# A decoder layer in fp32: first maxima and last cross attention as 32-row tiles, one pool of PSUM banks, a new order of steps

## What is computed

```python
def attn(x):                       # self attention, causal; q, k, v and the output have biases
    scores = einsum('bntd,bnsd->bnts', q, k) / sqrt(8)
    scores = where(causal, scores, -inf)
    return softmax(scores) @ v @ Wp + bp
def xattn(x, ctx, mask):           # cross attention to 77 rows, masked
    scores = where(mask, -1e9, einsum('bhqd,bhkd->bhqk', q, k) / sqrt(8))
    return softmax(scores) @ v @ Wo.T
def ffn(x):                        # weights of the two best of 8 experts, from softmax(gate)
    y = einsum('bsd,edf->bsef', x, expert_W) + expert_b
    return einsum('bsef,bse->bsf', y, comb) / 2
x = x + attn(layernorm(x)); x = x + xattn(layernorm(x), ctx, mask); x = x + ffn(layernorm(x))
```

## Time and profile before

| | us |
|---|---|
| median of 3 runs | 418.57 (415.2 to 419.45) |
| the profiled execution | 416.35 |
| its span | 414.6 |

### The profile page before, as it was taken

One profiled execution on the slowest core, in us unless ns is written; L12 is line 12 of the kernel. 1 busy time (PEld: TensorE's weight loads), 2 busy tenths in 40 slices (PEclk: granted clock), 3 DMA queues, 4 the chain that ended last, 5 costly groups with the idle time before them and its releaser, 6 DMA issues. The chain is left out here.

```text
span 414.6 us, 6303 instructions
## 1 busy us (share of the span) xinstructions
PE 333.7 (80%) x2204; PEld 156.2 (38%) x2204; DVE 266.5 (64%) x655; ACT 178.0 (43%) x339; POOL 134.2 (32%) x199
## 2 busy tenths in 40 slices
PE   5944868999975498799879898997988859688883
PEld 1421423444442144346434443553442344332440
DVE  5835886786882288367999864897461268631377
ACT  1400243566575065587540577664059612018100
POOL 6550041232254031004538500332961123900014
PEclk9895786999999599899899989999799977769998
DMA  6861174000035320001541000002110002110000
GB/s 142 163 73 28 41 101 61 5 2 2 2 64 86 44 40 5 4 0 37 87 74 36 28 6 2 2 2 41 38 29 4 1 2 48 28 30 2 0 2 25
DMA packets 19637, 14.40 MB, mean 35 GB/s; under 512 B 2461, under 2 KB 19605, under 8 KB 19605
## 3 DMA queue, kind: packets, MB, share of 16 engines
q1 hardware_dynamic: 19149, 13.60, 18.6%
q10 hardware_dynamic: 456, 0.39, 0.4%
HBM read 2.45 MB, written 1.05 MB: 8 GB/s over the span
## 5 line engine op out<-in xcount | busy, mean ns | idle before, releaser
L788 DVE TENSOR_REDUCE peaks<-peak_ps 128x1 f32<-128x512 f32 (+3 forms) x176 | 106.8, 638 | 61.8 <-PE peak_ps L988 60.2
L692 ACT ACTIVATE probs<-unit_ps 128x512 f32<-128x512 f32 x160 | 87.6, 600 | 85.9 <-PE unit_ps L1025 85.5
L599 POOL TENSOR_SCALAR_AFFINE_SELECT probs<-probs 128x512 f32<-128x512 f32 (+1 forms) x80 | 43.9, 551 | 150.4 <-ACT probs L692 150.4
L988 PE MATMUL peak_ps<-k_stack,q_stack 96*128 96x512 bf16 (+2 forms) x192 | 68.4, 383 | 0.0
L979 PE MATMUL peak_ps<-causal,ident_b 128*128 128x128 bf16 (+2 forms) x176 | 47.7, 271 | 25.2 <-DMA k_stack<-parts_k 8.5
L1025 PE MATMUL unit_ps<-q_stack,k_stack 102*128 102x512 bf16 (+3 forms) x256 | 56.7, 309 | 4.2 <-ACT probs L692 1.9
L1040 PE MATMUL mix_ps<-probs,v_s 128*9 128x256 f32 (+3 forms) x512 | 45.8, 454 | 1.6 <-POOL probs L599 1.6
L979 PEld LDWEIGHTS peak_ps<-causal,ident_b 128*128 128x128 bf16 x176 | 17.7, 101 | 63.4 <-DVE peaks L788 37.4
L610 POOL TENSOR_TENSOR yw<-yw 128x512 f32<-128x512 f32 (+2 forms) x42 | 34.3, 816 | 17.2 <-DVE yw L876 13.9
L700 ACT ACTIVATE xprobs<-unit_ps 77x512 f32<-77x512 f32 x64 | 33.8, 594 | 11.0 <-PE unit_ps L1048 11.0
L1094 PE MATMUL unit_ps<-expert_w_s,normed_t 128*128 128x512 f32 x64 | 35.5, 673 | 1.6 <-DVE yw L876 1.3
(11 more groups left out here) (134 smaller groups left out, 407.8 us busy)
## 6 DMA issues: line engine op xcount, KB each, us to landing
q_stack<-parts_q SPq DMA_DIRECT2D x24, 128.0 KB, 3.9
k_stack<-parts_k SPq DMA_DIRECT2D x48, 64.0 KB
xq_stack<-parts_x SPq DMA_DIRECT2D x24, 128.0 KB, 3.8
state<-in_x SPq DMA_DIRECT2D x4, 256.0 KB, 5.7
out<-state SPq DMA_DIRECT2D x4, 256.0 KB, 2.3
expert_w_s<-in_expert_w SPq DMA_DIRECT2D x1, 512.0 KB, 5.6
xk_stack<-parts_x SPq DMA_DIRECT2D x12, 38.5 KB
q_stack<-peaks_t ACTq DMA_DIRECT2D x16, 12.0 KB
```

Of the source, the lines that this page charges most:

```text
L599: gp.affine_select(out=v, in_=v, compare_op=ALU.is_ge, fill=0.0, base=0, pattern=pattern, channel_multiplier=-1).then_inc(causal_done, 1)
L692: ac.activation(probs[:, grp % 2, u, :], unit_bank(step), ACT.Exp, scale=SCALE).then_inc(unit_taken[UNIT[step] % UNITS], 1)
L788: ve.tensor_reduce(dst, peak_bank(step)[:, 0:n * width].rearrange("p (h k) -> p h k", h=n), X_AXIS, ALU.max, negate=True).then_inc(peak_ta ...
L988: last = te.matmul(dst, q, keys, start=False, stop=(i == len(heads) - 1), skip_group_check=True)
```

## The change

- **Batch 0's maxima** (`TILED_PEAKS`) are made in fp32 without stacks. Weights in another column order (`wk_ts`, `wq_ts`, loaded first) put one head in each of four 32-row groups, with four groups of heads interleaved by 8 rows. ACT copies the projected keys once (`k_t`) and the projected queries four times (`q_t`), each time scaled by `own`, which is 1 on the 8 rows of the head that is meant and 0 elsewhere. `tile_peak` is then a matmul over 32 partitions, lane j = partitions 32j to 32j + 31, to a bank of its own; the causal bias is added by four bf16 matmuls of `pick` and `causal_rows`. There are 48 such steps and 64 reduces on DVE. The projections with their stacks are still made for the scores.
- **Batch 3's cross attention** (`TILED_CROSS`) has no stacks at all: `project_xt`, `tile_xpeak` (16 steps, four products of 77 columns each, one reduce), `turn_tile_xpeaks` (4, one for each group of four heads: PE turns the maxima, DVE adds them into a spare row of `xq_t`) and `tile_xscores` (16, fp32 over 32 rows). `context_tile` makes its keys once, early.
- **The mask** is -2^30, exact in bf16, in one row instead of three; 4 DMAs and five DVE instructions fewer.
- **Banks.** All eight PSUM banks are one pool; the planner gives each step its bank (`PLACE`), with a semaphore pair for each bank. `AHEAD` limits how many steps of a kind may be in flight in the plan.
- **The planner** has a new table of costs by engine, follows the four row tiles, banks and stacks, and takes from eight chains, `scores`, `experts`, `cross`, `scale`, `peaks`, `prepare`, `attend`, `context`, by the earliest start and then by that rank.
- **At the start** POOL clears `k_stack[:, 0]` only after the first x has been turned, DVE makes `lanes`, `pick` and `own` from the identity, `causal` is built before the steps, the weights for batch 0's tiles are loaded first, and warm matmuls write bank 7.

The core of the diff:

```diff
-UNITS, PEAK_BANKS = 3, 2
+BANKS, WARM_BANK = 8, 7
+TILE = 32
+SPARE = (16, 16, 0, 0)
+TILED_PEAKS, TILED_CROSS = 0, B - 1
+TILE_PEAKS = (((0, 0), (1, 128)), ((2, 0),), ((3, 0),))
+AHEAD = {'peak': 4, 'tile_peak': 3, 'xpeak': 2, 'tile_xpeak': 5, 'scores': 2, 'xscores': 5, 'tile_xscores': 5, 'expert': 5}
-ORDER = ("cross", "peaks", "experts", "prepare", "attend")
+ORDER = ('scores', 'experts', 'cross', 'scale', 'peaks', 'prepare', 'attend', 'context')
...
+LATENCY, HOP, SWITCH, RANK, ISSUE = 0.22, 0.05, 0.0, 0.0, 0.62
+        if kind in STACKS:
+            n, *counts = STACKS[kind]
...
+            for r, count in zip(ready, counts):
+                free["dma"] = max(free["dma"], r) + ISSUE * count
+            done[("stacked", -1 if kind == "split_context" else b, n)] = free["dma"] + 2.2
...
+                fit = [i for i in usable if bank_free[i] <= start]
+                i = max(fit, key=lambda i: bank_free[i]) if fit else min(usable, key=lambda i: bank_free[i])
+                bank_uses[i] += 1
+                place[step] = (i, bank_uses[i])
...
 SP, split_k of batch 0
                         wait_cleared(sp, "k_stack")
+                        for i in range(2):
+                            for s in range(2):
+                                r = MAX_ROW + 3 * s
+                                sp.dma_start(k_stack[r:r + 3, i, s], ones).then_inc(ones_stacked, 16)
...
 POOL
+                elif kind == "turn_x" and (b, k) == (0, 0):
+                    wait_taken(pool, step)
+                    gp.memset(k_stack[:, 0].bitcast(F32), 0.0).then_inc(cleared, 1)
...
 ACT
+                elif kind == "project_qt":
+                    act.wait_ge(bias_ready, 1)
+                    wait_full(act, step)
+                    for i in range(GROUPS):
+                        ac.activation(q_t[:, i], bank_of(step), ACT.Identity, bias=q_bias[:, i:i + 1],
+                                      scale=own[:, i:i + 1]).then_inc(q_ready if i < 3 else taken_of(step), 1)
...
 DVE
+                elif kind == "tile_peak":
+                    grp, i, j = k
+                    p, s = divmod(4 * grp + j, 2)
+                    wait_full(dve, step)
+                    for t, col in TILE_PEAKS[i]:
+                        last = ve.tensor_reduce(peaks[:, p // 4, t, p % 4, s:s + 1],
+                                                bank_of(step)[:, col:col + 128 * (t + 1)], X_AXIS, ALU.max, negate=True)
+                    last.then_inc(taken_of(step), 1)
+                elif kind == "turn_tile_xpeaks":
+                    wait_full(dve, step)
+                    ve.tensor_tensor(xq_t[:, k], xq_t[:, k], bank_of(step), ALU.add).then_inc(taken_of(step), 1)
...
 PE
+            def bank_free(step):
+                i, n = PLACE[step]
+                if i == WARM_BANK and n == 1:
+                    pe.wait_ge(causal_ready, 1)
+                if n > 1:
+                    pe.wait_ge(bank_taken[i], n - 1)
...
+                elif kind == "tile_peak":
...
+                    for c in range(4):
+                        te.matmul(diagonal, lane(pick, j)[:, 128 * c:128 * c + 128],
+                                  lane(causal_rows, j)[:, c].unsqueeze(1).broadcast_to([TILE, len(TILE_PEAKS[i]), 128]),
+                                  start=(c == 0), stop=False, skip_group_check=True)
+                    for t, col in TILE_PEAKS[i]:
+                        last = te.matmul(bank[:, col:col + 128 * (t + 1)], lane(q_t, j)[:, grp, 128 * t:128 * t + 128],
+                                         lane(k_t, j)[:, 0:128 * (t + 1)],
+                                         start=False, stop=(t, col) == TILE_PEAKS[i][-1], skip_group_check=True)
+                    last.then_inc(full_of(step), 1)
+                elif kind == "tile_xscores":
+                    grp, j = divmod(k, 4)
+                    if j == 0:
+                        wait_taken(pe, ("turn_tile_xpeaks", b, grp))
+                    bank_free(step)
+                    te.matmul(bank_of(step)[0:S2], lane(xk_t, j)[:, KEYS_OF[grp]], lane(xq_t, j)[:, grp],
+                              start=True, stop=True).then_inc(full_of(step), 1)
```

More of the change, by code:

```diff
@@ L178, in plan, with has_bank @@
+    return n.get(kind, lambda: [])()
+STACKS = {"split_q": ("q", 3, 2, 1), "split_k": ("k", 6, 4, 2), "split_xq": ("x", 3, 2, 1), "split_context": ("x", 6, 4, 2)}
 def plan():
     left = {name: list(steps) for name, steps in chains().items()}
-    ready = dict.fromkeys(ORDER, LOADED)
-    free = dict.fromkeys(("pe", "act", "dve", "pool", "dma"), 0.0)
-    banks = {"misc": [0.0] * 2, "unit": [0.0] * UNITS, "peak": [0.0] * PEAK_BANKS}
-    done, turned, norms, steps = {}, set(), [], []
+    free = dict.fromkeys(("act", "dve", "pool", "dma"), 0.0)
+    tiles, issue, mode = [0.0] * 4, 0.0, None
+    bank_free, bank_uses = [0.0] * BANKS, [0] * BANKS
+    done, begun, place, steps, norms, turned = {}, {}, {}, [], [], set()
+    ahead = {kind: [] for kind in AHEAD}
+    loaded = {("ln_stats", b, 0): (4.0, 13.0, 15.0, 17.0)[b] for b in range(B)}
+    loaded[("context_keys", 0, 0)] = 15.0
+    first, last = ("tile_peak", 0, (0, 0, 0)), ("tile_xpeak", B - 1, (3, 3))
+    def has_bank(step):
+        return cost(step)[0] and not (step[0] == "values" and step[2][1])
@@ L191, in plan @@
             kind = step[0]
-            pe, engine, busy, _ = cost(step)
-            if any(x not in done for x, _ in needs(step)):
+            if any(x not in done for x in needs(step)):
                 continue
@@ L197, in plan @@
                 continue
-            start = max([ready[name]] + [done[x] + delay for x, delay in needs(step)])
-            ring = ring_of(kind)
-            if ring:
-                start = max(start, min(banks[ring]))
-            start = max(start, free["pe"])
-            if best is None or start < best[0]:
-                best = (start, name, step, ring)
-        start, name, step, ring = best
+            pe = cost(step)[0]
+            start = max([loaded.get(step, 0.0)] + [done[x] for x in needs(step)])
@@ new lines, in plan @@
+            if pe:
+                tile = tile_of(step)
+                start = max(start, issue, max(tiles) if tile is None else tiles[tile])
+                if has_bank(step):
+                    usable = range(BANKS - (first not in done or last in done))
+                    start = max(start, min(bank_free[i] for i in usable))
+                if kind in AHEAD and len(ahead[kind]) >= AHEAD[kind]:
+                    start = max(start, ahead[kind][-AHEAD[kind]])
+            switch = bool(pe) and (tile_of(step) is None) != (mode is None)
@@ L206, in plan @@
+            key = (start + SWITCH * switch + RANK * rank, rank)
+            if best is None or key < best[0]:
+                best = (key, start, name, step)
+        _, start, name, step = best
         kind, b, k = step
-        pe, engine, busy, then = cost(step)
+        pe, work = cost(step)
         left[name].pop(0)
-        idle = int((start - free["pe"] - WARM_SLACK) / WARM_TIME)
-        if (("peak", 0, (0, 0)) not in done or ("split_xpeaks", B - 1, 0) in done) and idle > 0:
-            steps.append(("warm", len(steps), idle))
+        t = start
@@ new lines, in plan @@
+        if pe:
+            mode = tile_of(step)
+            idle = int((start - max(issue, max(tiles)) - 0.5) / 0.5)
+            if (first not in done or last in done) and idle > 0:
+                steps.append(("warm", len(steps), idle))
+            tile = tile_of(step)
+            t = start + pe
+            if tile is None:
+                tiles, issue = [t] * 4, t
+            else:
+                tiles[tile], issue = t, start + 0.05
+            t += LATENCY
+        made = []
+        for engine, busy, lag in work:
+            begin = max(free[engine], t)
+            free[engine] = begin + busy
+            t = begin + busy + lag
+            made.append(t)
+            t = t + HOP if engine == "pool" else begin + busy
@@ L235, in plan @@
+        if kind == "take_mix":
+            bank_free[place[("values", b, (k, 0))][0]] = t
+        if kind in AHEAD:
+            ahead[kind].append(t)
         if kind == "ln_norm":
@@ L712, in _ @@
+                    ac.copy(mixed_t[:, k], bank_of(step)).then_inc(taken_of(step), 1)
                 elif kind == "choose":
```

948 lines of the change are left out of this document (539 added, 409 removed).

## The result

The changed kernel takes 430.09 us (median of 4 runs, 426.95 to 431.62) against 419.01 of the kernel before beside it: 1.0275 times as long, with a 95% interval of 1.0185 to 1.0365. Its span is 429.6 us, 15 more than before, at a mean clock of 0.833 against 0.897. I had predicted 365 with a range of 338 to 398.

What follows compares the result with a forecast made beforehand. Nothing was at its limit from end to end: a stack-bound head, a middle with PE 87% busy, a one-chain tail. 414.6 - 24 - 18 - 11 = 361.6 us of span, 365.3 us as measured time, range 338 to 398.

Steps and rivals of the forecast that it cites:

- Head: Start of the kernel: batch 0's maxima without stacks let scores and batch 1 begin earlier, 24 us gained, bounds 15 and 33.
- 15.6 for all, half of DVE's, so it hides: Head: PE needs 3.9 us per four heads of batch 0's maxima, 15.6 in all, hidden under DVE's 31.2.
- Tail: Last batch's cross attention to the end: no x-query stacking and maxima turned by group, 18 us gained, bounds 8 and 28.
- 0.56 (maxima): Tail: PE's time for one group of cross maxima, within 3.9 us of PE work per group.
- the first cross scores come 3.5 us after the first maximum: Tail: maxima turned group by group shorten this from 14.4 us to 3.5, saving 10.9.
- four groups cost 4 us more: Tail: maxima running inside the cross attention lengthen each group from 2.92 to 3.9 us, if tiles run together.
- Middle: Between head and tail: one pool of eight banks lets PE run ahead, 11 us gained, bounds 15 lost and 30 gained.
- Switches: Tiling mode changes on PE: at most 48 at 0.25 us, 12 us, two thirds under DVE's pace in the head.
- Row tiles don't overlap: Rival, chance 0.08: batch 0's maxima cost PE up to 62 us, a tail group 8.3, total 399 us.
- The pool makes it slower: Rival, chance 0.09: PE waits in order for its planned bank while others are empty, time about 430 us.
- The middle becomes tight: Rival, chance 0.12: the middle's 33 us of idle and the cold stretches go nearly all, 342 us.
- my signs of being wrong: Batch 0's reduces wait for PE; a named bank often holds PE while others are free; last score no earlier than 305 us.

Runs made afterwards that it cites:

- e9: The changed kernel with the row-tiled queries and keys of both stages in bf16 instead of fp32: 388.8 us, 0.931 of the kernel before.
- e1: The changed kernel with batch 0's maxima and batch 3's cross attention back on stacks: 412.8 us, 0.986 of the kernel before.
- e6: e1 with the planner counting a stack as landed 6.9 us after its last issue, not 2.2: 398.5 us, 0.947 of the kernel before.
- e4: The changed kernel with three full-array bf16 products of 512 columns ahead of each four row-tiled steps: 435.4 us, 1.041 of the kernel before.
- e5: Matrix products alone, layer left out, row-tiled stretches between full-array fp32 ones: 32 records of 77 columns took 1.9 us at full clock, 3.7 at half.
- e15: Matrix products alone, layer left out, short and long forms on row tiles and full array: 77-column fp32 group 3.6 us on the full array.

## Why the prediction was wrong

**Head, predicted -24 us, measured +11.** The start came late, outside my bounds: the first tiled product at 15.8 against 12, and the first reduce at 17.1 against 12.4. The 3.6 us that x waits behind the warm matmuls aren't in my chain and are nearly all of it. The step that failed is "15.6 for all, half of DVE's, so it hides". A group of four heads was to cost PE 3.9 us; that holds when the form runs alone at full clock (three fours at 1.14 us). In the kernel a four takes PE 2.7 us at half clock, and scores and projections follow each: 3.7 us, some 11 to 12 a group. PE and not DVE set the pace, the 64 reduces ended at 83 us and not 48, and DVE was busy for 17.3 of the 32 us from 13 to 45, 0.54, where I had named over 0.9. From this the rest is late: the first score at 60 instead of 39, batch 1's first maximum at 88 instead of 58. That batch 0's stacks would be the next limit was never tested by the kernel: batch 1's last k copy was issued by 61.2, 26 us before its first maximum. The 6.9 us of landing that I took from the earlier trace rows are also uncertain, because four copies of ones into the same stack were issued behind the twelve, until 30.6.

**Tail, predicted -18 us, measured +36.** The x-query to its first use is 0.9 us, as predicted (1.2 against the 9.5 before). Then three terms failed. First, "0.56 (maxima)" for a group: I priced 308 fp32 columns by their columns, and the 32 weight loads alone are busy for 4.6 us. The first group takes 2.65 us and the later ones 4.8, together some 15 us more than I had. Second, "the first cross scores come 3.5 us after the first maximum": they come 350.7 - 335.5 = 15.2 us after the first product. The first reduce is released by POOL, after DVE has stood for 5.0 us: POOL clears the buffer of these maxima (L675) only behind the x-query, which isn't in my chain; then the second group, and batch 2's `add_attention` (2.1 us) with its turn stand ahead on PE. Third and largest, "four groups cost 4 us more". From the first cross scores to the residual add it was 17.1 us (371.4 to 388.5), would have been 21, and is 49.7 (350.7 to 400.4); before, and in the changed kernel:

```profile
388.51 0.69 DVE L829 TENSOR_TENSOR state<-misc_banks,state 128x512 f32<-128x512 f32 x1 [2.58 <-PE misc_banks L916]
```
```profile
385.53 4.35 PE L1304 MATMUL banks<-expert_w_s,normed_t 128*128 128x512 f32 x6
...
400.36 0.69 DVE L972 TENSOR_TENSOR state<-banks,state 128x512 f32<-128x512 f32 x1 [1.51 <-PE banks L1053]
```

In these 49.7 us lie two more groups of maxima, batch 2's gate and experts (L1304), and half clock for everything from 350 to 388 us. In e9 the same part takes 30.6 us. From the last self attention score to the x-query it takes 29 us and not 18, since batch 2's cross attention and experts stand there too. This is the work that left the middle: in e1, without tiles, the tail is already 113 us. So the tail of a stage cut at the last score is no measure of the last batch alone, and my 18 us were partly a matter of bookkeeping.

**Middle, predicted -11 us, measured -32.** The number flatters the forecast. PE is busy in the middle for 151 us where it was 178, a share of 85% in both and a clock of 0.93 in both: 27 of the 32 us are work that now lies in head and tail (1206 matmuls against 1343), and 5 us are less idle time. PE does meet a maximum's bank less often, but e1 gains 6 us in all by pool, order and mask, so my 11 for the middle was too much for this order; in e6's order the three together gain 20. The wait for batch 2's k_stack is there, at 3.9 us under the 5 I gave it; its last copy was issued by 135.8, so the landing took 7.6 us to the first use:

```profile
128.02 7.82 SPq L565 DMA_DIRECT2D k_stack<-parts_k  x12
...
143.40 0.58 PE L1167 MATMUL banks<-causal,ident_b 128*128 128x512 bf16 x1 [3.88 <-issue]
```

So PE is busy for 85% of the middle and not for 88 to 92%.

**Switches.** 0.25 us each, 12 us in all, most of it hidden. Measured 0.16 to 0.30 each; right in size, but not hidden, since PE was the slow side in the head. Up to 24 visits at 0.32 to 0.60 are 8 to 14 us. The sum had none of it.

**The rivals.** *Row tiles don't overlap* gave 62 us for the maxima and 8.3 for a tail group; measured 66 us (17 to 83) and 9. Its numbers came true and its mechanism is false: the tiles overlap, but they are slowed by half clock, by loads and by the work between. Its sum, 399 us, was still too low, as it left the head's and tail's other work at full clock. *The pool makes it slower* has the time (430) and the opposite mechanism. *The middle becomes tight* comes to 343 us and not 342. The clock was in no case: I read the earlier trace rows as saying that it falls where PE is idle. Two of my signs of being wrong came: the reduces of batch 0 wait for PE (31.8 us), and the last score is done at 306 us, not before 305.

## What to carry to other kernels

Price a matrix product by its weight loads and passes as well as its columns: 16 fp32 products of 77 columns cost 1.9 to 4.8 us of PE where their columns are worth half a microsecond, and in bf16 0.5. Before work is moved to an engine that seems half idle, add what the engine would have to do in that very stretch, at the lower clock too. One pool of banks was worth 25 us together with the order made for it, and an order made for a pool needs it. Check a planner's belief about when a transfer lands against the trace, and measure what a truer number brings: here it was 14 us in one order and nothing in another.

## What the hardware did that I had not expected

- TensorE was granted half clock with no idle time in the record, for 35.0 of 35 us in e4 and for 38 us in the changed kernel, the second by stage:

```profile
350.00:388.00 38.00, 38.00 (x157) 19.87 (x157) 14.66 (x54) 10.01 (x19) 1.02 (x1) 0.50 0.00 0
```

  Alone, short row-tiled fp32 products and a single row tile did it; fours of 512 columns, the maxima's form and short full-array products stayed at 1.00. In the kernel the maxima's form, with waits and scores between, ran at 0.50. In the tail the fall itself came behind a wait, at 341 us, after PE had been busy for 0.78 of 3 us; in e5 it came at 99 us with PE busy throughout. The Trainium skill (TensorE: Matmul & The Clock Gate, Part 1) says that the gate follows how busy the PE has been; the profile's busy share doesn't bear that out here. What decides stays open.
- A weight load on row tiles was paced at 59 ns at full clock and 115 at half in e5 and e15, at 150 at half in the kernel (4.80 us for 32), and on the full array at 111 at full clock (fp32, loads of 128 columns, a few records may be missing).
- Four row tiles of fp32 512 take 0.86 us together, as long as one product of the full array.
